# Four edits in an eight-stage attention and FFN program: a convolution tap on ScalarE, identity products around the decay heads, a later wait for global values

## What is computed

```
# attention with decay, 16 heads of 16, over 4 sequences of 1024
q = x @ W_q;  latent = (x @ W_k + x @ W_v) @ W_down;  k, v = latent @ W_up_k, latent @ W_up_v
scores = q.k / sqrt(256) * exp(-0.01 * |t1 - t2|);  out = softmax(scores) @ v @ W_o

# windowed attention, 16 heads: causal; same 64-block, or within 128 back, or keys 0..3 ("global")
out = softmax(mask(rope(q).rope(k) / 4)) @ v @ out_w.T

# gated recurrence, per channel, along t
i_raw, f_raw = conv4(x @ Wi, conv_i), conv4(x @ Wf, conv_f)     # causal, 4 taps, depthwise
f = sigmoid(f_raw);  i = silu(i_raw) * (1 - f);  h_t = f_t * h_(t-1) + i_t
out = (h * rsqrt(mean(h*h)) * g_norm * silu(x @ Wg)) @ Wo
```

## Time and profile before

| | us |
|---|---|
| median of three runs | 3180.8 |
| lowest and highest | 3168.49 and 3181.08 |
| the profiled execution | 3183.8 |
| its span, first to last instruction | 3182.0 |
| PE busy in the span | 2767.0 (87%) |
| DVE busy | 1928.7 (61%) |
| ACT busy | 1536.1 (48%) |
| POOL busy | 972.3 (31%) |
| mean granted TensorE clock | 0.92 of full speed |

### The profile page before, as it was taken

How to read it: one execution, slowest core, us unless ns; L and a number is a source line. 1 busy time by engine, 2 the same in 40 slices (tenths; PEclk the granted TensorE clock), 3 DMA queues, 4 the chain that set the end, 5 groups by cost and what they waited for, 6 DMA issues and landing times. The chain is left out here.

```text
span 3182.0 us, 47799 instructions
## 1 busy us (share of the span) xinstructions
PE 2767.0 (87%) x15657; PEld 1680.8 (53%) x15657; DVE 1928.7 (61%) x4279; ACT 1536.1 (48%) x2920; POOL 972.3 (31%) x1386
## 2 busy tenths in 40 slices
PE   8699999999997199997896199996959999988889
PEld 3244444444445089986553189996524554534443
DVE  7678888888826844443555844443966663527952
ACT  4257777777761055453212054453335554345544
POOL 4322222222201144453001144452463442120021
PEclk9679999999998599998997599998979999998889
DMA  8622222222214133433003033434353442100001
GB/s 290 233 61 64 73 74 64 78 70 66 72 46 150 39 91 85 97 75 77 14 0 133 27 93 89 92 76 95 89 142 90 105 110 76 48 1 1 0 7 47
DMA packets 185012, 249.76 MB, mean 78 GB/s; under 512 B 40904, under 2 KB 129736, under 8 KB 184800
## 3 DMA queue, kind: packets, MB, share of 16 engines
q1 hardware_dynamic: 153024, 212.12, 21.9%
q0 software_dynamic: 30720, 33.98, 6.5%
q10 hardware_dynamic: 1056, 1.02, 0.1%
HBM read 154.49 MB, written 90.92 MB: 77 GB/s over the span
## 5 line engine op out<-in xcount | busy, mean ns | idle before, releaser
L2054 DVE CUSTOM_DVE_ANT_0 s0Ah_SD<-s0Ah_ps_s,s0Ah_table 128x1024 f32<-128x1024 f32 x512 | 607.2, 1222 | 155.4 <-PE s0Ah_ps_s L2112 155.4
L2078 ACT ACTIVATE s0Ah_PM<-s0Ah_ps_x 128x512 f32<-128x512 f32 x1024 | 530.7, 602 | 191.8 <-PE s0Ah_ps_x L2137 100.5
L2112 PE MATMUL s0Ah_ps_s<-s0Ah_plus_k,s0Ah_plus_q 48*128 48x512 f32 x1024 | 424.9, 479 | 24.7 <-DMA s0Ah_plus_k<-s0A_parts 20.9
L2034 POOL TENSOR_TENSOR s0Ah_DG<-s0Ah_SD,s0Ah_mx 128x128 f32<-128x128 f32 x512 | 204.5, 400 | 553.3 <-DVE s0Ah_mx L2054 553.3
L2112 PEld LDWEIGHTS s0Ah_ps_s<-s0Ah_plus_k,s0Ah_plus_q 48*128 48x128 f32 x1024 | 168.2, 194 | 274.3 <-DVE s0Ah_mx L2054 177.7
L2157 PE MATMUL s0Ah_ps_v<-s0Ah_PM,s0A_V 128*17 128x512 f32 x2048 | 273.6, 607 | 0.0
L2137 PE MATMUL s0Ah_ps_x<-s0Ah_plus_q,s0Ah_plus_k 50*128 50x512 f32 (+3 forms) x640 | 238.5, 389 | 0.0
L2332 DVE CUSTOM_DVE_ANT_0 s4Ch_SD<-s4Ch_ps_s,s4Ch_table 128x264 f32<-128x264 f32 x448 | 168.2, 429 | 93.3 <-PE s4Ch_ps_s L2413 90.7
L2137 PE MATMUL s0Ah_ps_x<-s0Ah_minus_q,s0Ah_minus_k 50*128 50x512 f32 (+3 forms) x640 | 220.0, 392 | 0.0
L2361 ACT ACTIVATE s4Ch_PM<-s4Ch_ps_x 128x512 f32<-128x512 f32 (+1 forms) x256 | 131.1, 564 | 124.2 <-PE s4Ch_ps_x L2440 124.1
L2146 PE MATMUL s0Ah_ps_x<-top_ident,s0Ah_DG 128*128 128x128 f32 x512 | 169.7, 331 | 0.0
(11 more groups left out here) (455 smaller groups left out, 6604.3 us busy)
## 6 DMA issues: line engine op xcount, KB each, us to landing
s1W_raw_w<-in_L_ffn_w SPq DMA_DIRECT2D x16, 1024.0 KB
s3W_raw_w<-in_L_ffn_w SPq DMA_DIRECT2D x16, 1024.0 KB
s0A_parts<-s0Ap_sp_top SPq DMA_DIRECT2D x24, 512.0 KB
s0A_parts<-s0Ap_sp_rest SPq DMA_DIRECT2D x24, 512.0 KB
s0Ah_plus_q<-s0A_parts SPq DMA_DIRECT2D x64, 128.0 KB, 2.6
s0Ah_plus_k<-s0A_parts SPq DMA_DIRECT2D x64, 128.0 KB, 3.0
s0Ah_minus_q<-s0A_parts SPq DMA_DIRECT2D x64, 112.0 KB, 2.6
s0Ah_minus_k<-s0A_parts SPq DMA_DIRECT2D x64, 112.0 KB, 2.7
```

Of the source, the lines that this page charges most:

```text
L2034: nc.gpsimd.tensor_tensor(DG[p % 3][:, r * TB + t, :], SD[i % NSD][:, t * P:(t + 1) * P], mx[p % 3][:, r * TB + t:r * TB + t + 1].to_broad ...
L2054: nc.vector.tensor_tensor_reduce(SD[i % NSD][:, :], ps_s[i % 2][:, :, :].rearrange("p a n -> p (a n)"), table[:, (TB - 1 - t) * P:(TB - 1 ...
L2078: nc.scalar.activation(PM[n % NPB][:, :], ps_x[u % NX][:, :], ACT.Exp).then_inc(e_ok, 1)
L2112: x = nc.tensor.matmul(ps_s[i % 2][:, half, :], q[at(r), t * P:(t + 1) * P], k[at(r), half * GT:(half + 1) * GT], start=True, stop=True)
```

## The change

Four edits. Line numbers of the changed kernel are 3 to 9 higher behind the first edit.

1. In the recurrence the newest tap moves from DVE to ACT: ACT multiplies the projection, as it stands in PSUM, by the tap's weight and writes `CV`, ahead of each copy into `RAW`; DVE starts from that with the three older taps.
2. `OM` is gone. DVE makes (FG - 1) * SI in one SCALAR_TENSOR_TENSOR; the sign that this turns over is turned back by a negated norm weight, `against`, made once.
3. Identity products: 12 at the end of PE's stream in `project_latent`, 10 at the start of PE's stream in `heads_decay`, and one of half the width after each of the 30 steps of `score` ahead of the main loop.
4. In `heads_window` PE's wait for `globals_in` moves from ahead of the main loop to the first `global_values`.

```diff
@@ gated_recurrence, DVE
-                        nc.vector.tensor_scalar(CV[:, s, c, :], RAW[:, s, c, 0:GT], w[:, c, 0:1], None, ALU.mult)
-                    for k in range(1, K):
-                        dve.drain()
+                    for k in range(K - 1):
+                        if k:
+                            dve.drain()
                         for c in range(DC):
                             i = nc.vector.scalar_tensor_tensor(CV[:, s, c, :], RAW[:, s, c, k:k + GT],
                                                                w[:, c, k:k + 1], CV[:, s, c, :], ALU.mult, ALU.add)
...
-                dve.wait_ge(act_ok, START + (g + 1) * 3 * DC)
-                    nc.vector.tensor_tensor(SI[:, c, :], SI[:, c, :], OM[:, c, :], ALU.mult).then_inc(i_ok, 1)
+                dve.wait_ge(act_ok, START + (g + 1) * 2 * DC)
+                    nc.vector.scalar_tensor_tensor(SI[:, c, :], FG[:, c, :], 1.0, SI[:, c, :],
+                                                   ALU.subtract, ALU.mult).then_inc(i_ok, 1)
@@ gated_recurrence, ACT
+                act.wait_ge(act_ok, START + g * 2 * DC)
                         act.wait_ge(raw_mm, START + g * 2 * DC + n * DC + c + 1)
+                        nc.scalar.activation(CV[:, s, c, :], ps[:, c, :], ACT.Copy, scale=w[:, c, K - 1:K])
                         nc.scalar.copy(RAW[:, s, c, K - 1:], ps[:, c, :]).then_inc(raw_ok, 1)
...
-                act.wait_ge(act_ok, START + g * 3 * DC + DC)
-                for c in range(DC):
-                    nc.scalar.activation(OM[:, c, :], FG[:, c, :], ACT.Copy, bias=1.0, scale=-1.0).then_inc(act_ok, 1)
@@ project_latent, end of PE's stream
+            keep_dense(nc, ident, ps_t[:, 0, :], 12)
@@ heads_decay, PE
+            keep_dense(nc, ident, ps_x[NX - 1][:, :], 10)
             for i in range(AHEAD):
                 for half in range(2):
                     score(i, half)
+                nc.tensor.matmul(ps_x[NX - 1][:, 0:2 * P], ident[:, :],
+                                 ident[:, :].unsqueeze(1).to_broadcast([P, 2, P]), start=True, stop=True)
@@ heads_window, PE
             def global_values(p):
+                if p == 0:
+                    pe.wait_ge(globals_in, 16 * 4)
...
             pe.wait_ge(hide_ok, START + 1)
-            pe.wait_ge(globals_in, 16 * 4)
             for p in range(NP):
```

10 lines of the change are left out of this document (6 added, 4 removed).

## The result

The kernel after takes 3158.71 us (median of five runs, 3150.45 to 3201.53) against 3180.8 us before (3168.49 to 3187.03). The ratio is 0.9937, with a 95% interval from 0.9916 to 0.9957: about 20 us less. A second series of the same code gave 3158.39 us (nine runs, 3146.34 to 3194.8), ratio 0.9935 [0.9914, 0.9955]. The forecast was 3145 with a range from 3129 to 3168: the sign and the range held, and the gain came out at 22 us instead of 36.

A forecast was written before the change was run, and what follows sets the result against it. Bounds: PE's half clock and DVE's maxima early in the decay heads, PE's wait for VG, DVE's and ACT's circles in the recurrence. 12.7 + 10.7 + 12.4 = 35.8 us off 3183.8 gives 3148.0, median 3145; range 3129 to 3168.

The forecast's parts named there:

- a decay part worth nothing (3158): Case within the forecast's high end of 3168: the decay heads' 12.7 us gain does not come.
- Identity products, front: Ahead of the decay heads' steps: 24 rows at full clock take 10.7 us, end at 120.3; cost +0.2 us.
- Between the steps: Decay heads' 30 steps: products hide under DVE's 1.19 us maximum, PE needing 1.03 us a step; 2.4 us less.
- The main loop's start: Decay heads: first twelve steps run at full clock, 1.47 us each; 10.5 us less.
- my discount of 1.5: Main loop's start in the decay heads: 12.0 us cut to 10.5 because pipeline filling hardly gets shorter.
- Rival 4: Decay heads: clock drops once, at the engines' meeting or in the steps, and returns; half the gain, 3151; chance 0.07.
- Rival 1: Decay heads: clock falls during the 30 steps, 2.03 us each, +22.5 us; 3180, no change; chance 0.11.
- Rival 2: Decay heads: clock never comes up because identity products don't count as work; 39.7 us lost, 3197; chance 0.03.
- The wait for VG: Window heads: main loop starts earlier once the wait moves to first use; 10.7 us less, between 9.5 and 11.0.
- The tap and OM: Recurrence: DVE saves 1.7 us a turn, period 20.6 us; 12.4 us less, bounds 5 and 14.5.
- DVE's own circle: Recurrence: DVE's turn without its waits for ACT, taken as 22.0 us, becomes 20.3.
- Rival 3: Recurrence: ACT's circle becomes the bound, L745 every 21.5 us, gain only 5 us; 3152; chance 0.14.

The follow-up runs named there:

- f_first: Kernel after with ScalarE's order changed in the recurrence, the forget input's taps and copies ahead of the squares: 3148.2 us, ratio 0.9906.
- no_steps: Kernel after without the identity product behind each of the 30 steps, the 12 and 10 in front kept: 3162.63 us, ratio 0.9948.
- 3162-us execution: Profiled execution of the unaltered kernel after, from its second series: 3161.95 us.
- 3202-us execution: Profiled execution of the unaltered kernel after, from its first series: 3202 us.
- narrow_steps: `f_first` with 128 columns in place of 256 in the identity product behind each of the 30 steps: 3170.11 us, ratio 0.9968.
- tap_only: Kernel before with only the newest tap of both convolutions on ScalarE, the `1 - f` products kept: 3190.49 us, ratio 1.0027.
- recurrence_alone: Kernel before with the new recurrence (tap, `f - 1`, `against`) and nothing else: 3161.53 us, ratio 0.9955.

## Why the prediction was right, and where it was not

**Why the number fell inside the range.** The high end took in "a decay part worth nothing (3158)", and that is what came. The forecast itself, with its chance of 0.65, had all three parts paying, and one did not in most runs. So the range held, and two of the three parts; the path to 3145 did not.

**Identity products, front.** The clock part held: 0.92 over the stretch from 110 to 130.5. The 24 rows were priced at full clock, 10.7 us, with an end at 120.3. Their last one starts at 120.9:

```profile
L164 PE MATMUL s0Ap_ps_t<-top_ident x24: 593/593/1057, 109.2 to 120.9; 128*128 128x512 f32 x24
```

The clock was at 0.50 from 109.9 to 113.3, under the first of them, so they take 12.3 us; in `f_first`, where it did not fall, 10.6. The phase starts at 122.3 instead of 121.9 and the first score at 131.49 instead of 130.56: 0.9 and not 0.2. The last product in front of it ends at 131.20, and the score then waits 0.29 us for its rows.

**Between the steps.** The first step that failed is the sum for PE, 0.59 + 0.44 = 1.03 us. By their starts score and product take 0.66 + 0.63 = 1.29, more than DVE's 1.19, which was itself too high: alone DVE does a step in 1.15. So the products do not hide under DVE; they are the bound, as the next width shows too (1.50 with 384 columns). Without them a full clock would have saved time here: the first steps of `no_steps` take 1.15 us where before had a mean of 1.27. With them 30 steps take 38.8 us, and the -2.4 became +0.3. With the later start the main loop begins at 170.25 instead of 169.05: +1.2.

**The main loop's start.** The second and larger one, -10.5 us. The mechanism was right: with the clock up throughout (`f_first`), 39 tiles of PM stand between 169 and 198.7 where there were 24, and the heads take 803.6 us; against the later start the loop gives 12.0, even without my discount of 1.5. What I did not ask is whether the clock, once up, stays up when the loop begins. I had one stretch in which the loop ran at full clock, and took it for proof that the loop holds it. In five traces it falls 3 to 5 us into the loop, and in three of them it comes back near 199; so in the 3162-us execution the loop gains 1.8 us, and the later start takes 1.2 of it. Rival 4 had a drop on the way, at the meeting of the engines or in the steps, and half of the gain left; it came in the loop and took nearly all. Why it comes there is open.

**Rival 1**, the clock falling during the steps, is real: it is the 3202-us execution. There the step takes 2.30 us and not 2.03, since the half-width product takes 1.15 us at half clock and not 0.85, and the main loop, begun at 200.6, needs until 230.4 to get its clock. In the traces of `no_steps` and `narrow_steps`, without the product and with half of it, the clock falls in the steps; at its full size it held in five of six. Rival 2 didn't occur; the clock came up under the products in front in eight of the nine traces that have them, and in the ninth, `f_first`, it was up already.

**The wait for VG.** Right: 10.2 us in the kernel after, 10.5 alone, forecast 10.7. The wait of 0.2 us left at L2472 isn't seen; SP issues VG's copies 27.4 us into the phase and before 27.7, and the first reader at 2391.6, 33.4 us into the phase, finds them landed. Before, the wait for them ended 33.3 us in, so this is as close as the forecast had it.

**The tap and OM.** 11.2 us for 12.4, period 20.79 for 20.6. The nearness is in part luck: no turn takes 20.6. Turns with the clock up take 19.94 to 20.12, less than the 20.3 that I had for DVE's own circle, and the others 21.0 to 22.2, more than the 20.95 at the far end. The term that was mis-sized is ScalarE's extra work. The tap takes 0.69 us and not the 0.59 of a copy, and four of them do not hide under PE's quarters, because ScalarE comes to them late from the squares and then runs all eight without a pause. PE waits up to 1.5 us behind them, and in three turns the clock falls there, so that the gate projection takes 1.5 to 2.6 us longer. That fall had no term. `f_first`, which changes the order alone, has no such wait and takes 4 to 6 us back. Rival 3 (ScalarE's circle becomes the bound) is what `tap_only` shows; in the kernel after it is what turns 1 to 3 show, and in the 3202-us execution, where every gate projection was slow, the period of 21.60 is its 21.5.

**The sum.** With the clock up through the loop the profiled sum would have been right within 2 us a term: `f_first` less its own edit is 3146.7 + 4.0 = 3150.7, and five of fourteen runs of the kernel after lie at 3146 to 3152. Seven lie at 3157 to 3169; of those the traced one has lost 9.8 us in the heads against `f_first`. The last two, at 3195 and 3202, are slower than the kernel before.

## What to carry to other kernels

Fill work that holds TensorE's clock must be priced in the case where it fails too: here the same products gave 10.8 us or cost 30, and products of half the width were worse than none. When a resource comes up earlier, look at what the next stage does to it before its gain goes into the sum, and price a small product by the distance of two starts, beside the instructions it will run between. Half of a wide one's time gave 0.44 us here, the starts gave 0.63, and the filler became the bound. Two edits on two engines that share a circle have no prices of their own: try both alone, and when work is moved onto an engine, look at its order there. And look at single turns before a mean period is taken for one mechanism.

## What the chip showed that I had not expected

The same instructions gave three courses of the granted clock: in the kernel after, full until 134.8, until 174.8, or, by `f_first`, through the whole of the heads. Without the products one trace (`recurrence_alone`, whose edit lies 2600 us further on) had the rise at 177.9 and the four others at 197.8 to 199.2. So a whole-kernel ratio of 0.2 to 0.5% here can be clock alone.

Even with PE listed as busy for all of 171.1 to 174.4 us, the clock fell at 174.4.

A wait of PE of 2.65 us in the recurrence was followed by a projection of 6.58 us instead of 3.68, so the price of a wait isn't its length. Before, the slow projection was that of f, behind waits of 2.8 to 5.4 us; but in turns 4 and 5 of the kernel after a wait of 3.0 us stands ahead of one that takes 3.69.

GpSimd's operation on 128x4 elements took 0.67 us beside a DVE tap and 0.20 us without.
